# A graph network with residual norms on one core: the correction, the loop and the rings of a build block are placed anew

## The reference

```python
edge_index = jnp.stack([src, dst])
x = _layernorm(x + L0(x, edge_index, edge_weight, weight, bias))     # segment_sum((x @ W)[src] * w, dst) + b
x = _layernorm(x + L1(x, edge_index, edge_type_2, basis1, att1, ...)) # two gated relational layers
x = _layernorm(x + L2(x, edge_index, W, b))                          # normalised by degree
x = _layernorm(x + L3(x, edge_index, edge_attr_8, Wq, bq, ...))      # attention over edges, 8 heads
```

## Time and profile before

| | us |
|---|---|
| median of 3 runs | 1253.46 |
| lowest, highest | 1247.01, 1256.37 |
| the profiled execution | 1259.67 |
| its span in the trace | 1257.9 |
| PE busy (share of the span) | 1181.3 (94%) |
| DVE busy | 851.3 (68%) |
| ACT busy | 437.1 (35%) |

### The profile page before, as it was taken

The page is one execution under the profiler, slowest core; times in us unless marked ns, Lnnn a source line. Parts: engine busy times, 40 slices in busy tenths (PEclk is TensorE's granted clock), DMA queues, the critical chain, the costliest instruction groups (busy, mean ns, idle before and its releaser), DMA issues.

```text
span 1257.9 us, 21464 instructions
## 1 busy us (share of the span) xinstructions
PE 1181.3 (94%) x8083; PEld 540.5 (43%) x8084; DVE 851.3 (68%) x1330; ACT 437.1 (35%) x586; POOL 307.6 (24%) x220
## 2 busy tenths in 40 slices
PE   6987879999999999999999999999999899999997
PEld 2333334323344334345445454455333365555553
DVE  7575657544434555553368875575999889899997
ACT  2444546512122222112311002216553255444454
POOL 2000000000010133344655655545556000000000
PEclk9988989999999999999999999999999899999999
DMA  8567867598799789753122213112223376565653
GB/s 327 209 217 247 297 224 269 151 407 305 243 363 307 257 285 314 278 165 109 2 35 35 50 19 69 2 3 33 34 33 67 139 235 231 202 220 187 213 186 112
DMA packets 64325, 222.73 MB, mean 177 GB/s; under 512 B 31138, under 2 KB 36002, under 8 KB 48272
## 3 DMA queue, kind: packets, MB, share of 16 engines
q1 hardware_dynamic: 34706, 156.38, 35.8%
q0 software_dynamic: 25184, 53.10, 16.7%
q10 hardware_dynamic: 4350, 12.07, 2.8%
HBM read 198.92 MB, written 59.92 MB: 206 GB/s over the span
## 4 chain that ended last, share of the span: by engine, by line
PE 69%; DVE 11%; issue 7%; DMA 7%; ACT 3%; SPq 2%; DVEq 1%; ACTq 0%
PE PS L1853 26%; PE PS L1802 10%; PE PS L1727 6%; PE PS L1657 5%; PE PS L2098 4%; PE PS L2085 4%; DMA R<-R 4%; DVE R L1172 4%; DVE R L1209 4%; PE PS L1675 3%; PE PS L1967 2%; PE PS L2144 2%; PE PS L1889 1%; PE PS L1773 1%; DMA W<-in_basis_s 1%
## 5 line engine op out<-in xcount | busy, mean ns | idle before, releaser
L812 POOL DMA_INDIRECT bias_d<-R x160 | 271.0, 1694 | 331.3 <-DMA bias_d<-R 220.5
L1853 PE MATMUL PS<-R 128*128 128x512 f16 x1300 | 298.1, 381 | 0.0
L1853 PEld LDWEIGHTS PS<-R 128*128 128x128 f16 x1300 | 120.5, 98 | 180.6 <-issue 49.7
L1727 PE MATMUL PS<-R,XX 125*128 125x512 f16 (+2 forms) x612 | 134.7, 354 | 15.3 <-ACT R L1400 6.8
L1613 ACT ACTIVATE R<-PS 128x1024 f32<-128x1024 f32 (+1 forms) x100 | 106.2, 1087 | 109.6 <-PE PS L2085 77.9
L1802 PE MATMUL PS<-W,XX 128*128 128x512 f16 x600 | 136.0, 386 | 5.1 <-DVE R L1010 2.7
L926 DVE TENSOR_SCALAR R<-W,R 125x1250 f16<-125x1250 f16 x160 | 89.4, 606 | 53.7 <-PE PS L1727 39.4
L1172 DVE CUSTOM_DVE_ANT_0 R<-PS,R 128x1250 f16<-128x1250 f32 x80 | 116.8, 1459 | 5.5 <-PE PS L2021 2.9
L2098 PE MATMUL PS<-R 128*32 128x256 f32 (+1 forms) x1600 | 102.5, 391 | 5.2 <-DVE R L1209 5.2
L2085 PE MATMUL PS<-R 128*128 128x256 f16 (+3 forms) x800 | 99.6, 275 | 5.4 <-ACT R L1613 2.2
L779 POOL DMA_DIRECT2D bias_d<-bias_d x39 | 21.6, 556 | 324.0 <-PE PS L1727 164.2
(11 more groups left out here) (231 smaller groups left out, 1411.0 us busy)
## 6 DMA issues: line engine op xcount, KB each, us to landing
bias_d<-bias_d POOLq DMA_DIRECT2D x39, 1280.0 KB, 9.0
R<-in_basis_s SPq DMA_DIRECT2D x32, 1024.0 KB, 6.9
W<-in_basis_s SPq DMA_DIRECT2D x28, 1024.0 KB, 6.1
W<-bias_d SPq DMA_DIRECT2D x27, 1024.0 KB, 4.9
XX<-bias_d SPq DMA_DIRECT2D x13, 1024.0 KB, 4.9
R<-key_d SPq DMA_DIRECT2D x20, 500.0 KB, 4.0
R<-R SPq DMA_DIRECT2D x120, 80.0 KB, 5.9
W<-bias_d SPq DMA_DIRECT2D x7, 904.0 KB, 4.6
```

The costliest lines, as they stand in the source:

```text
L812: pool.indirect_dma_start(bias_d, bass.IndirectOffsetOnAxis(ap=idx[:, c:c + 1], axis=0), attr[:, c, :], None, bounds_check=DUMP + GC * P - ...
L1727: ins = T.matmul(mm_out(3 * (j % 2) + b, p1 - p0), own[0:EC, bass.ds(c, 1), :, :].rearrange("p c m w -> p (c m w)"), hots(p0, p1), start=f ...
L1853: ins = T.matmul(mm_out(SUM_BANK(s, i), D), lhs, rhs, start=n == 0, stop=n == len(terms) - 1)
```

## The change

- In `build` PE does fixed visits 0 and 1, then the correction of the block before, fixed visit 2, the loop, `load_range`, fixed visit 3. So the correction comes behind six matmuls, where it came behind the loop and four of the fixed visits' matmuls, and visit 1 is not split any more.
- In `make` DVE makes selections 0, 1 and 2, then the loop's, `load_range`, selection 3.
- The ring `more` has four places instead of two. It lies in R3, from where `key` was, and takes that column's room and the support tail's; `zero` lies at its start.
- `key` (the number that DVE compares in every selection) and the tail of the support move to W, behind the other build constants. The tail now overlaps the columns that ACT's first mixed weights (M0) are written to; ACT waits for `sup_kept` there.

```diff
-MORE = 2
+MORE = 4
@@ tiles
-        zero = r3[:, NT * D + 2 * NN + CH:NT * D + 3 * NN + CH]
-        more = zero.bitcast(F16).rearrange("p (s r) -> p s r", s=MORE)
-        key = r3[:, NT * D + 2 * NN:NT * D + 2 * NN + CH]
+        key = in_w(CH)
+        sup_tail = in_w(4 * D // 2)
+        o = NT * D + 2 * NN
+        assert o + MORE * NN // 2 <= RELS * FT * NN
+        zero = r3[:, o:o + NN]
+        more = r3[:, o:o + MORE * NN // 2].bitcast(F16).rearrange("p (s r) -> p s r", s=MORE)
@@ SUPS, DVE's copy of the support
-                [r3[:, o + k * D // 2:o + (k + 1) * D // 2].bitcast(F16) for k in range(4)]]
+                [sup_tail[:, k * D // 2:(k + 1) * D // 2].bitcast(F16) for k in range(4)]]
...
-                          r3[:, NT * D + 3 * NN + CH:NT * D + 3 * NN + CH + 4 * D // 2].bitcast(F16)).then_inc(sup_kept, 1)
+                          sup_tail.bitcast(F16)).then_inc(sup_kept, 1)
@@ make (DVE)
                 dve.wait_ge(built, t4 * 4 + (j + 1))
-                fixed(0)
+                for m in range(FIXED - 1):
+                    fixed(m)
                 with dve.Fori(begin, end) as c:
...
                 load_range(dve, ranges[(j + 1) % 2], t4 * 4 + (j + 1))
-                for m in range(1, FIXED):
-                    fixed(m)
+                fixed(FIXED - 1)
@@ mixed_high (ACT)
+                if m == M0:
+                    act.wait_ge(sup_kept, 2)
@@ build (PE)
                 pe.wait_ge(evicted, t4 * 4 + (j + 1))
-                fixed(0)
+                for m in range(2):
+                    fixed(m)
+                if j:
+                    fix(t4, j - 1)
+                elif not first:
+                    fix(t4 - 1, 3)
+                for m in range(2, FIXED - 1):
+                    fixed(m)
                 with pe.Fori(begin, end) as c:
...
-                fixed(1, range(1))
-                if j:
-                    fix(t4, j - 1)
-                elif not first:
-                    fix(t4 - 1, 3)
-                fixed(1, range(1, 3))
-                fixed(2)
                 load_range(pe, ranges[(j + 1) % 2], t4 * 4 + (j + 1))
-                for m in range(3, FIXED):
-                    ins = fixed(m)
-                ins.then_inc(built, 1)
+                fixed(FIXED - 1).then_inc(built, 1)
```

More of the change, by code:

```diff
@@ L164, in gnn_resnorm @@
         assert o <= 6 * NN // 2 + NN // 4
-        o = NT * D + 3 * NN + CH
         SUPS = [[w_b[:, k * D // 2:(k + 1) * D // 2].bitcast(F16) for k in range(NT)],
                 [w_b[:, (NT + k) * D // 2:(NT + k + 1) * D // 2].bitcast(F16) for k in range(6)] +
-                [r3[:, o + k * D // 2:o + (k + 1) * D // 2].bitcast(F16) for k in range(4)]]
-        assert o + 4 * D // 2 <= RELS * FT * NN
+                [sup_tail[:, k * D // 2:(k + 1) * D // 2].bitcast(F16) for k in range(4)]]
         wst_first = r1f[:, NT * NN // 2 - 4 * D:NT * NN // 2].bitcast(F16).rearrange(
```

## The result

The changed kernel takes 1259.64 us (median of 20 runs, 1257.24 to 1266.15), the kernel before 1252.64 (20 runs, 1243.11 to 1259.23). The ratio is 1.007 with a 95% interval of 1.0048 to 1.0093. The medians are 7.0 us apart and the means 8.8; the interval allows 6 to 12 us, under 1%. The fastest run is 14 us slower than before, the slowest 7: the change takes more from the fast end.

A forecast was written before the change was run, and what follows sets the result against it. Build was taken as paced by its block rhythm and late stores. Rhythm +15, stores -9 and -3 gave +3, leaned to +4: 1263.7 from the profiled 1259.67, 1257 against the median 1253.46; range 1246 to 1268.

The forecast's parts named there:

- The cycle moves: Build: the binding cycle leaves block start, correction, second copy; a block takes 4.18 us against 3.81, +15 us over 40 blocks.
- The signs that were named: Build: first copies 4.2 us apart, PE idle 0.5 to 0.6 ahead of last visit, store waits under 10 in all.
- Its size: Build rhythm: 4.18 us a block against 3.81, +0.37 each, +15 us over 40 blocks.
- That the sequencer stops at the correction's wait: PE's sequencer in build: its lead is zero at the correction's start, so loop and load_range both follow, taking 2.17 us.
- the bound of 3.62: Build: lower bound of a block if none of the sequencer's work shows, -0.19 us a block, -7.6 in all.
- The stores: First copy's waits for stores in build, 18.3 us: slower blocks take off 9, a less full DMA queue 3 more.
- the rest of the stage: Build: the 18.3 us of store waits fill what 156.8 us of block rhythm leaves of 175.1.
- The sequencer is ahead: Rival, build: blocks take 3.62 us, -7.6, with a little given back to stores: -4, 1249 us; chance 0.15.
- It does nothing: Rival, build: the loop's exit costs little behind queued matmuls, some 3.8 us a block, stores as before: 1253 us; chance 0.10.
- The stores stay as late: Rival, build: bursts of zeroing make stores late, no wait shrinks, DMA waits stay above some 14 us: +15, 1268; chance 0.15.
- Ring, tiles, wait at M0: Ring of four, moved tiles and ACT's new wait at its first mixed weights: 0 us each; the last 0.69 at most.

The follow-up runs named there:

- e1: The changed kernel with PE's load_range moved between fixed visit 1 and the correction: 1249.18 us, ratio 0.9978 to the kernel before.
- e5: The changed kernel with PE's load_range done twice in a row where it stands: 1280.47 us, ratio 1.026 to the kernel before.
- e6: The kernel before with PE's load_range done twice in a row where it stands, behind the correction: 1249.43 us, ratio 1.001.
- e3: The kernel before with the build's 24 zeroing transfers issued behind the build: 1318.61 us, ratio 1.0558.
- e4: The changed kernel with the build's 24 zeroing transfers issued behind the build: 1335.63 us, ratio 1.0701 to the kernel before.
- e8: e1 with the build's zeroing released over 36 blocks instead of 32: 1240.93 us, ratio 0.9941 to the kernel before.
- e11: e8 with four zeroing transfers moved ahead of the build, 20 instead of 24 left in it: 1245.62 us, ratio 0.9956 to the kernel before.
- e2: The changed kernel with PE's old order within a block put back, all else as changed: 1252.34 us, ratio 1.001 to the kernel before.
- e7: The changed kernel with the ring of loop selections back at two places: 1261.29 us, ratio 1.0093 to the kernel before.
- e10: e8 with one matmul of visit 2 moved ahead of the correction, so seven stand ahead: 1245.12 us, ratio 0.9968 to the kernel before.

## Why the prediction was right

*The forecast*, 1257 within 1246 to 1268 and "the same within 1%", against 1259.64 and a ratio of 1.007. The time is in the range and 2.6 us above the forecast. Some of the closeness is luck: against the profiled execution the rhythm came out 2 us dearer than summed and the stores gave back 3 us more, and the two cancel.

*The cycle moves* from the second copy to "correction, loop, load_range, last visit, first copy". The signs that were named came: gap ahead of the last visit, first copy waiting for PE nearly always (38 of 40), second copy waiting 0.9 (0.89), idle at the correction (0.4 predicted, 0.27 to 0.36 in the late blocks, though only at 29 corrections). The gap was predicted as 0.5 to 0.6 and is mostly 0.39 to 0.47. The prediction counted 0.57 from the end of streaming, and the rows count from the last matmul's end, which it had put 0.17 later: 0.40 in the rows. In the block whose correction starts at 211.64 the last visit starts 2.15 behind it, where the sum had 2.17. Shown by experiment: e1 and e5 change only load_range's place or number, and the block's length follows; e6 shows it all but free in the old place.

*Its size.* Predicted 4.18 a block, +0.37, +15 us; measured 4.25 in the quiet stretch, and +17.1 by e3 and e4, 0.44 a block. The undersized term is in part the table read: I took one block's 298 ns, and the reads of after go from 295 to 507 ns:

```profile
L466 PEldq TENSOR_LOAD <-W x40: 295/308/507, 69.4 to 242.9; - x40
```

Their median is 308, but 37 of them, read out one by one, have a mean of 329, so the long ones add 0.03 a block. Before, a read lay behind the correction with the array busy. The rest of the 0.07 is not assigned to a step.

*That the sequencer stops at the correction's wait.* Right, and it decided the sign. In the block shown above the loop is entered at 216.1 and load_range at 217.2, both behind the correction's wait, which ended at 215.91. Blocks came 4.25 apart, and 3.62 apart in e1, e8 and e11, where no table read is left behind the loop. The rule of the Trainium skill that was weighed ("Advanced Engine Details and Errata", "Sequencer and Instruction Queues") has an instruction wait for its semaphore in the engine's queue. By it the bound of 3.62 would have held; the trace does not agree.

*The stores.* I took 18.3 us of waits, let 12 of them go and expected 6 to stay: 4.4 stayed. From profile to profile the sum was +4 and the copies show +2.7. The flaw is the last step, from the profile to the median. I took +4 off the profiled execution, 6.2 above the median, as if the change were worth the same in any run. But the profiles of before's rhythm differ by their late stores. Three with PE's old order and a rhythm of 3.81 to 3.83 have 9.3, 16.9 and 18.3 us of waits, copies of 159.1, 167.8 and 169.9, and spans of 1244.7 (e6), 1255.7 (e2) and 1257.9 (before). What lies outside the copies is nearly the same in all profiles with the zeroing in the build (1082 to 1089 us), except e11. A typical run has less to give back than the profiled one had, while the 17 us of rhythm come in full. An estimate: the median of before, 1252.64, lies a little under half way from e6's profiled run (1246.45; late stores cost it 159.1 - 152.6 = 6.5) to before's (1259.67; 17.3), so about 11.6 us are late stores in it. With 2.9 left after the change that gives 17.1 - (11.6 - 2.9) = +8.4, against 7.0 by the medians and 8.8 by the means. It would also fit the narrower scatter of after (9 us between its ends against 16). That late stores make up the scatter of single runs is inferred; no profile of a median run was taken.

That longer blocks mean fewer waits is borne out by the three profiles with blocks of 4.2 us and more (4.4, 2.3 and 0 us: after, e7, e5) against four with blocks of 3.6 to 3.8 and the same zeroing (18.3, 16.9, 9.3 and 8.6: before, e2, e6, e1). One profile of each can't put these four in an order.

*The clock, which the sum left out.* Two late stores in the profiled execution of before cost more than the wait. PE, idle for 4.40 and 5.66 us at the correction, went on at a granted clock of 0.50, the lower of its two levels (1.2 GHz). The second row is the stretch from 106 to 110 us, and its third number from the end is that clock:

```profile
105.48 1.22 PE L1711 MATMUL PS<-R,W 128*128 128x512 f16 x3 [4.40 <-ACT R L1398]
106.00:110.00 4.00, 4.00 (x13) 1.69 (x12) 0.40 (x1) 1.70 (x2) 0.31 (x1) 0.50 0.26 62
109.53 1.24 ACT L1398 ACTIVATE R<-PS 128x1280 f16<-128x1280 f32 x1 [1.47 <-PE PS L1727]
...
179.54 1.22 PE L1711 MATMUL PS<-R,W 128*128 128x512 f16 x3 [5.66 <-ACT R L1398]
180.56 5.08 PE L1727 MATMUL PS<-R,XX 125*128 125x512 f16 x15
```

Three correcting matmuls took 1.22 instead of 0.69, and the first copy behind each long wait came 5.34 us behind the last one, where the same blocks of e3 take 3.92: 1.4 us each, 2.8 of the 17.3. After the change the granted clock is 1.00 from 76 to 244 us; e6 has no such stretch in the build either, e2 has two. So the 18.3 us of waits were not simply "the rest of the stage": some of them cost nothing, and the clock cost something, and that the two figures matched was partly chance. The clock also bears on the scatter. Of the 23 runs of before beside e1 to e4, the two longest (1258.72 and 1258.30) have the lowest mean granted clocks, 0.981 and 0.979, and the shortest (1244.25) has the highest, 0.989; the profiled one has 0.982. That fits the longest times being those with long store waits, though a run's mean does not say where its clock was low.

*Rivals.* "The sequencer is ahead" is refuted by the 4.25. "It does nothing" likewise. "The stores stay as late" is refuted by 4.4 us where it needed over 14; e3 shows that the lateness comes from the zeroing beside the build, as it said, but slower blocks do mend it.

*Ring, tiles, wait at M0.* Nothing, as said: e7 and e2. ACT's first mix waits for PE only (1.8 us). Behind the build the shift passes on one to one: from the last first copy to the end of the span it is 1015.8 us before and 1015.2 after.

*Open:* why e1, e8 and e10 gain less in the median than in the profiled build. Waits that differ from run to run are the likely cause, but one profile of each kernel does not show how they are distributed.

## What to carry to other kernels

Register and branch work was free here only while PE had matmuls queued in front of it, and nothing was queued ahead across PE's wait at the correction. So do table reads and address work ahead of a wait that stands anyway, and not between a loop and the instruction that closes the critical cycle. Count for each cycle between engines both the array's time and the sequencer's, and take the larger. Where a stage also waits for transfers in some runs, a slower rhythm hides part of its own cost: size such a term against a typical run, not against the one that was profiled, and look at the granted clock behind each long wait.

## What the runs showed of the hardware that I had not expected

- A table read into a register on PE's sequencer takes 295 to 507 ns with the same kind of operands, so a path over it has a spread of 0.2 us a block.
- Doing load_range twice in a row adds 0.60 us. A single one takes about 0.8 from its first sequencer row (212.9) to the last visit's (213.7). Part of the difference may be that the second one needs less: in e5 four table reads on PE between 205 and 215 us come with only two FUSED_REGOPS rows of their line.
- A store of 80 KB or less beside the zeroing can take 12 to 15 us: the build's own up to 12.3, with the DMA engines 0.79 busy on average, and a mixed-weight store 15.20 with them 0.95 busy. With the zeroing gone the build's stores take 2.0 to 2.1 us (median, e3), and none of the 120 was waited for.
- A wait that leaves PE idle for 4 to 6 us can cost its own length and, here, 1.4 us more in the next block, at a granted clock of 0.50.
